# Splitting the k.k products from row 6 on into two f16 parts, in a fused feed-forward and delta-rule attention kernel

## What is computed

```
h = silu(tlin(x, w1)) * tlin(x, w2)            # 256 -> 1024
h = gelu(tlin(h, h1)); h = gelu(tlin(h, h2))   # 1024 -> 1024, weights -1, 0, 1, scaled by row
x = x + 0.5 * tlin(h, w3)                      # 1024 -> 256

k = k / max(norm(k), 1e-6)
for t in range(1024):                          # per batch and head, S is 16 x 16
    retrieval = S @ k[t]
    S = S + outer(beta[t] * (v[t] - retrieval), k[t])
    o[t] = S @ q[t]
x = x + o @ w_out + b_out
```

## Time and profile before

| what | us |
|---|---|
| median of three runs | 1911.45 (1910.48 to 1912.49) |
| the profiled execution | 1912.61 |
| its span, first to last instruction | 1910.6 |
| PE busy | 1789.6 |
| POOL busy | 1239.6 |
| DVE busy | 1167.3 |
| ACT busy | 1069.4 |
| granted TensorE clock, mean | 0.989 of full speed |

### The profile page before, as it was taken

One profiled execution on the slowest core, in us unless ns is written; L12 is line 12 of the kernel. 1 busy time (PEld: TensorE's weight loads), 2 busy tenths in 40 slices (PEclk: granted clock), 3 DMA queues, 4 the chain that ended last, 5 costly groups with the idle time before them and its releaser, 6 DMA issues.

```text
span 1910.6 us, 28212 instructions
## 1 busy us (share of the span) xinstructions
PE 1789.6 (94%) x9674; PEld 1064.2 (56%) x9674; DVE 1167.3 (61%) x2729; ACT 1069.4 (56%) x2049; POOL 1239.6 (65%) x1458
## 2 busy tenths in 40 slices
PE   5999989999999899998999989999799999998999
PEld 4865545555655455554655545455455555554577
DVE  5154666767766676665666656567667777776330
ACT  5656465465655664646556465554646556645455
POOL 6554584667584856748476594856758567658564
PEclk9999989999999999999999999999999999999999
DMA  7000000000000000000000000000000000000000
GB/s 292 23 1 1 1 1 1 1 1 2 0 2 1 23 1 23 1 1 1 1 23 0 1 1 1 23 1 1 1 1 1 1 1 12 1 12 1 1 12 12
DMA packets 5261, 23.06 MB, mean 12 GB/s; under 512 B 640, under 2 KB 1664, under 8 KB 3584
## 3 DMA queue, kind: packets, MB, share of 16 engines
q1 hardware_dynamic: 5120, 21.26, 3.0%
HBM read 17.06 MB, written 4.19 MB: 11 GB/s over the span
## 4 chain that ended last, share of the span: by engine, by line
PE 57%; POOL 23%; issue 8%; DVE 7%; ACT 4%; DMA 0%; POOLq 0%; ACTq 0%; SPq 0%; DVEq 0%
PE ffn_bank L1013 36%; POOL hid_lo L514 8%; POOL hid L523 6%; PE att_bank L1061 4%; PE att_bank L1051 4%; PE att_bank L1033 4%; POOL pairs L549 4%; POOL pairs_lo L557 3%; PE ffn_bank L996 2%; PE ln_bank L966 2%; PE state_bank L1069 2%; PE att_bank L1078 1%; ACT hid L642 1%; DVE qk_u L834 1%; DVE roots L772 1%
## 5 line engine op out<-in xcount | busy, mean ns | idle before, releaser
L1013 PE MATMUL ffn_bank<-hid_hi,w_sb 128*128 128x512 f16 (+1 forms) x2592 | 899.3, 358 | 27.9 <-ACT hid L629 17.7
L1013 PE MATMUL ffn_bank<-hid_lo,w_sb 128*128 128x512 f16 (+1 forms) x2592 | 898.6, 358 | 0.0
L514 POOL TENSOR_TENSOR hid_lo<-hid,hid_hi 128x512 f16<-128x512 f32 (+1 forms) x432 | 454.2, 1067 | 314.0 <-ACT hid_hi L613 313.8
L1013 PEld LDWEIGHTS ffn_bank<-hid_hi,w_sb 128*128 128x128 f16 x2592 | 263.3, 102 | 252.4 <-ACT hid L629 22.5
L549 POOL TENSOR_TENSOR pairs<-KQ 128x32 f32<-128x32 f32 (+15 forms) x496 | 327.2, 673 | 112.0 <-DVE KQ L797 72.9
L1013 PEld LDWEIGHTS ffn_bank<-hid_lo,w_sb 128*128 128x128 f16 x2592 | 255.3, 99 | 231.0 <-issue 30.6
L613 ACT CAST hid_hi<-hid 128x512 f16<-128x512 f32 (+1 forms) x432 | 231.7, 572 | 104.8 <-POOL hid L523 103.8
L642 ACT ACTIVATE hid<-ffn_bank,par_sb 128x512 f32<-128x512 f32 (+1 forms) x288 | 168.3, 635 | 148.4 <-PE ffn_bank L1013 147.5
L834 DVE TENSOR_TENSOR qk_u<-att_bank,U_sb 128x32 f32<-128x32 f32 (+15 forms) x256 | 111.3, 435 | 186.9 <-PE att_bank L1049 185.4
L996 PE MATMUL ffn_bank<-xn_hi,w_sb 128*128 128x512 f16 (+1 forms) x576 | 202.0, 360 | 16.3 <-ACT gate L624 8.9
L557 POOL TENSOR_TENSOR pairs_lo<-pairs,pairs_hi 128x32 f16<-128x32 f32 (+15 forms) x256 | 181.8, 714 | 36.7 <-ACT pairs_hi L690 36.6
(11 more groups left out here) (83 smaller groups left out, 2179.0 us busy)
## 6 DMA issues: line engine op xcount, KB each, us to landing
NK<-in_w SPq DMA_DIRECT2D x11, 1024.0 KB, 6.7
X<-in_x SPq DMA_DIRECT2D x7, 512.0 KB, 3.5
out<-X SPq DMA_DIRECT2D x7, 512.0 KB, 2.6
wqkvb_sb<-in_wqkvb SPq DMA_DIRECT2D x1, 1024.0 KB, 8.0
X<-in_x SPq DMA_DIRECT2D x2, 256.0 KB, 2.7
out<-X SPq DMA_DIRECT2D x2, 256.0 KB, 2.1
wout_sb<-in_wout SPq DMA_DIRECT2D x1, 256.0 KB, 8.9
par_sb<-in_par SPq DMA_DIRECT2D x1, 24.0 KB, 2.4
```

The lines of the kernel that those rows point to most:

```text
L514: pool.tensor_tensor(hid_lo[layer % 2][:, m, call.cols], hid[:, u % 3, call.cols], hid_hi[layer % 2][:, m, call.cols], ALU.subtract).then_ ...
L1013: mm = nc.tensor.matmul(ffn_ps(call, j), weight(name, kk, 2 * pair + i), v[:, kk, cols], start=kk == 0 and part == 0, stop=kk == KT_FF - 1 ...
```

## The change

Rows 6 to 15 of the k.k products go the way of the q.k products: they are made 9 ticks ahead instead of 4, cast by ACT, subtracted by POOL, and multiplied in two f16 matmuls by a new f16 matrix of minus ones. Rows 1 to 5 stay as they are. At one tick POOL now makes the pairs of split dots before those of unsplit ones. The buffers are the same.

```diff
+KK_SPLIT = 6
-SPLIT = {use: q for q, use in enumerate(u for u in DOTS if u[0] == "qk")}
+SPLIT = {use: q for q, use in enumerate(u for u in DOTS if u[0] == "qk" or u[2] >= KK_SPLIT)}
...
+        head_minus16 = sb("head_minus16", [P, P], F16)
...
-            pool.wait_ge(side_ready, 3)
+            pool.wait_ge(side_ready, 4)
...
-                for what, lead in PAIR_LEAD.items():
+                for whole, lead in ((False, PAIR_LEAD["qk"]), (True, PAIR_LEAD["kk"])):
                     for dot in dots_at(f, e + lead):
-                        if dot[0] == what:
+                        if (dot not in SPLIT) == whole:
                             make_pairs(dot)
...
+            nc.vector.tensor_scalar(head_minus16[:, :], head_ones[:, :], -1.0, None, ALU.mult).then_inc(side_ready, 1)
...
-                    i = SPLIT[dot]
-                    nc.tensor.matmul(ps[:, 0:n], head_ones16[:, :], pair(pairs_hi, i, dot), start=True, stop=False)
-                    nc.tensor.matmul(ps[:, 0:n], head_ones16[:, :], pair(pairs_lo, i, dot), start=False, stop=True).then_inc(att_filled, 1)
+                    i, ones = SPLIT[dot], head_ones16 if dot[0] == "qk" else head_minus16
+                    nc.tensor.matmul(ps[:, 0:n], ones[:, :], pair(pairs_hi, i, dot), start=True, stop=False)
+                    nc.tensor.matmul(ps[:, 0:n], ones[:, :], pair(pairs_lo, i, dot), start=False, stop=True).then_inc(att_filled, 1)
```

More of the change, by code:

```diff
@@ L724, in _ @@
             nc.vector.tensor_copy(head_ones16[:, :], head_ones[:, :]).then_inc(side_ready, 1)
+            nc.vector.tensor_scalar(head_minus16[:, :], head_ones[:, :], -1.0, None, ALU.mult).then_inc(side_ready, 1)
             dve.wait_ge(consts_ready, 2)
-            dve.wait_ge(side_ready, 3)
+            dve.wait_ge(side_ready, 4)
             nc.vector.memset(u_ps, 0.0).then_inc(u_zeroed, 1)
@@ L1108, in _ @@
             pe.wait_ge(masks_ready, 2)
-            pe.wait_ge(side_ready, 3)
+            pe.wait_ge(side_ready, 4)
             pe.wait_ge(u_zeroed, 1)
```

## The result

| | before | after |
|---|---|---|
| median of four runs, us | 1911.97 (1910.48 to 1913.47) | 1949.51 (1946.35 to 1949.60) |
| the profiled execution | 1912.61 | 1949.43 |
| its span | 1910.6 | 1947.7 |

The changed kernel takes 1.0192 times as long, interval 1.0175 to 1.0210. It is slower, as forecast, but the time lies above the range, 3.5 us over its upper end and 21.5 us over the value. A few executions of the study (one of e1, one of the kernel before) ran in a much slower state of the chip, at a lower granted clock; they are left out of all ratios and ranges.

A forecast was written before the change was run, and what follows sets the result against it. PE was taken as the bound on average, POOL in frames 3 and 13. To the profiled 1912.61 us the terms -0.7 + 0.2 + 2.6 - 0.4 + 1.5 + 12 add +15.2, giving 1928; range 1907 to 1946.

The forecast's parts named there:

- frame 6, from row 6 on: `xn_lo` stands in front of row 15's subtraction, so only row 15's own gain is left: -0.4 us.
- frame 4, from row 6 on: `xn_lo` stands in front of row 12's subtraction and delays PE, while rows 13 to 15 give 1.1: +1.5 us.
- frames 3 and 13: POOL is the bound there; the added subtractions delay PE's first q.k dot by some 6 us each, 12 us for both.
- PE's gain: Splitting k.k rows 6 to 15 saves PE 2.80 us per part, 44.8 us in 16 parts.
- What is added: Ten subtractions per part on POOL, 135 us in all, and ten casts on ACT, 75 us in all.
- Row 11 behind `xn_lo`: Row 11's subtraction follows `xn_lo` at tick 74; in frames 7 to 10 row 11 comes 1.55 us later than before.
- The step that failed: Rows 11 to 15 give PE 1.73 us per frame after row 11, if POOL keeps up.
- Three new waits of POOL on PE: Makes of rows 7, 8 and 9 wait for buffers of rows 3, 4 and 5; costed at nothing.
- The Trainium skill's rule: GpSimd and VectorE exclude each other during `xn` in 14 frames: 26 us in all, sum 1954; weighed at no cost.
- The much slower one: Rival: POOL and ACT hold PE in every part, 2 to 3 us more each, 1960 us; chance 0.14.
- delays are given back: No-change rival: delays in k.k rows only shorten later q.k waits in w1 and w2, 1913 to 1916; chance 0.12.
- The faster one: Rival: PE keeps its gain outside frames 3 and 13, 1885 us, or 1905 with half of it; chance 0.12.

The follow-up runs named there:

- e1: The changed kernel with `xn_lo` moved on POOL to tick 87, behind all k.k pairs, in twelve frames (not -1 and 4): 1922.01 us, ratio 1.0036.
- e3: The kernel before, nothing split, with the pairs of k.k row 11 made 3 ticks ahead instead of 4, behind `xn_lo`: 1942.69 us, ratio 1.0149.
- e2: The kernel before with `xn_lo` moved to tick 87 in the same frames as e1, nothing else: 1912.59 us, ratio 0.9990.
- e6: The changed kernel with the k.k products of frames 3 and 13 left unsplit: 1936.97 us, ratio 1.0124.
- e5: The changed kernel with ten unread f16 matmuls of 352 columns ahead of PE's wait for row 11 in twelve frames: 1946.64 us, ratio 1.0176.
- e9: The kernel before with the same ten filler matmuls as e5 in front of row 11 in the same twelve frames: 1923.45 us, ratio 1.0049.
- e4: The changed kernel with POOL's k.k subtractions cut to 32 columns, PE's work unchanged: 1918.38 us, ratio 1.0015.
- e8: The changed kernel with `xn_lo` late as in e1 and only frames 0, 1, 2, 6 to 10 and 14 split: 1903.65 us, ratio 0.9950.
- e10: e8 with casts and subtractions of the split k.k rows one tick earlier: 1902.22 us, ratio 0.9935 against the kernel before.

## Why the prediction failed, step by step

The distances between starts of PE's dots in the two timelines split the 37.1 us between them (each row is rounded by itself). "Twelve frames" are here those with `xn_lo` at tick 74: -1, 0, 1, 2, 5, 7 to 12 and 14.

| piece, us | predicted | measured |
|---|---|---|
| row 6 to row 11, twelve frames | +25.0 | +25.7 |
| row 11 to the first q.k dot, the same | -22.9 | -10.1 |
| frame 6, from row 6 on | -0.4 | -1.1 |
| frame 4, from row 6 on | +1.5 | +2.2 |
| frames 3 and 13 | +12 | +11.2 |
| rows 1 to 6, all frames | 0 | +6.6 |
| all between these stretches | 0 | +2.7 |
| sum | +15.2 | +37.1 |

(25.0 is 4 x 1.55, 3 x 1.80 and 5 x 2.67; -22.9 is 12 x -1.73 and the two waits of 1.05 for row 12.)

**PE's gain** was right: 44.8 predicted, 43.7 to 45.0 by the two ways of counting. The records of f32 k.k matmuls fell from 480 to 160:

```profile
L1054 PE MATMUL att_bank<-pairs,head_minus 128*128 128x32 f32 (+4 forms) x160 | 30.7, 275 | 0.7 <-POOL pairs L551 0.7
```

**What is added** was forecast a little too high: POOL +128 for 135, ACT +64 for 75. The widest subtraction took 1198 ns in the mean of both uses, where the earlier trace rows had 1292 for q.k alone:

```profile
L559 POOL TENSOR_TENSOR pairs_lo<-pairs,pairs_hi 128x192 f16<-128x192 f32 x32 | 17.6, 550 | 0.0
L559 POOL TENSOR_TENSOR pairs_lo<-pairs,pairs_hi 128x480 f16<-128x480 f32 x32 | 38.3, 1198 | 0.0
```

**Row 11 behind `xn_lo`** was right in place and size, with 25.7 us for 25.0 in twelve frames. e1 removes it in the eleven of them that it changes, e3 makes it without the split (24.3 us), and e2 bounds what moving `xn_lo` does otherwise at some 2 us.

**Frames 3 and 13** were right: 11.2 us in the timelines and 12.5 by e6, for 12. The distance from row 6 to row 15 grew from 20.4 us to 27.4 and 25.6 there, and was 25.1 in frames 7 to 10.

**The step that failed** is the sentence "Rows 11 to 15 (2080 columns) then give 1.73 us, if POOL keeps up; its list up to row 15 comes out within 0.3 us of PE's demand", carried from frame 7 to the eleven other frames. It held to 0.05 us in frames 7 to 10, each -1.78. The other eight gave -3.0 together instead of -16.0. e5 divides the 12.8 us that are missing in the twelve. With the filler, the same rows give -14.9 in twelve frames:

- 4.8 us go with the filler. 4.1 of them are in frames 0, 1 and 14, where PE waits 2.6 to 4.4 us for row 11 in after and works on at 1.2 GHz, and where e5 has no half clock. The prediction has no term for this, though the table of before lists the mean clock, 0.989. Frame -1 looks the same (-0.9), but there row 11 itself comes 1.2 us later in e5, so nothing is gained, and e9 shortens its tail as much (-1.1) without a half clock in it; this part is not shown to be the clock's.
- The other 8 us stay with the full clock. In frames -1, 5, 11 and 12 row 12 comes 3.1 to 4.1 us after row 11 in e5, against 2.0 in frames 7 to 10. POOL's timeline shows why: in these four two `hid_lo` stand between the two subtractions, and in the other eight they do not. e1 and e4 agree in part: with `xn_lo` gone (e1) PE still waits 2.40 and 3.81 us for row 12 in frames 5 and 12, though not in frame 11, and with short subtractions (e4) still 1.13 us in frame 5. No run moved the two `hid_lo` themselves, so this is read from the traces and not tested. That order could have been read before the result; I had read it in frame 7 only. These four give -1.1 us in e5 where 4 x -1.73 = -6.9 was predicted, so 5.8 of the 8; the rest is spread over frames 0, 1 and 2.

The ledger's 27.7 us for the clock are thus not its price. Part of what the clock takes, PE would have waited for POOL in any case: e5 took 19.5 us off the clock's row, and only some 3 us, no more than the noise, came off the time, with some 17 us of work added (as e9 shows), which was to cost nothing under its wait. The four executions of after say the same: at a mean clock of 0.975 and of 0.979, 8 us apart in the ledger, two of them took 1949.43 and 1949.60 us.

**Rows 1 to 6** were left out of the sum, since they are not split, and a second step failed here: "Three new waits of POOL on PE come too ... I cost them at nothing". POOL's waits for PE's matmuls before a make went from 39.1 us in 25 to 63.6 in 34. In frame 7 the one for row 7 was 1.87 us and did cost nothing. In frame 6 it does not. Between rows 5 and 6 PE takes a matmul of the layer norm (`ln_bank`) that waits for POOL's `roots`. Before, then after:

```profile
830.29 1.26 POOL L495 TENSOR_TENSOR roots<-X 128x512 f32<-128x512 f32 x1
831.61 1.13 PE L966 MATMUL ln_bank<-roots,average 128*128 128x512 f32 x2 [1.05 <-POOL roots L495]
```
```profile
851.67 0.67 POOL L551 TENSOR_TENSOR pairs<-KQ 128x256 f32<-128x256 f32 x1 [0.96 <-PE att_bank L1054]
855.02 1.27 POOL L497 TENSOR_TENSOR roots<-X 128x512 f32<-128x512 f32 x1
856.35 2.05 PE L969 MATMUL ln_bank<-roots,average 128*128 128x512 f32 x2 [1.96 <-POOL roots L497]
```

In front of `roots` now stand the makes of two more rows, POOL's wait of 0.96 us for PE to let go of a buffer, and a subtraction. PE waits 1.96 us instead of 1.05, and 3.4 us at half clock come with it, which the doubled duration shows (2.05 for 1.13). The piece grew by 2.6 us; in e5, with the same wait and no half clock, by 0.9. In frame 4 PE's wait for the same step rose from 2.36 to 2.83 us, since one more make stands in front of it, and 6.8 us at half clock come with it instead of 3.4; the piece grew by 1.8. These two frames make 4.4 of the 6.6 us. Of the rest some may be no effect of the split: in e2 and e3, where nothing is split, rows 1 to 6 took 1.5 us more as well, 1.2 of it in frame -1. The 2.7 us between the stretches were not taken apart.

**The Trainium skill's rule** on GpSimd and VectorE (SBUF — State Buffer, "SBUF: two separate sides") was weighed at no cost. The subtraction of row 10 (width 320), begun at 984.39 beside VectorE's `xn` of 983.66 to 985.51, took 1.77 us in frame 7, where this width took 0.79 in the mean before:

```profile
984.39 1.77 POOL L559 TENSOR_TENSOR pairs_lo<-pairs,pairs_hi 128x320 f16<-128x320 f32 x1
```

PE waited 0.9 us for it in frames 7 to 10. In after that cost nothing, as row 11 set the time behind it. In e1 and e8 it is what is left: these frames gain 1.8 us where the split is worth 2.8. By the rule as the prediction priced it, 26 us would have come on top; the traces show about 1 us in such a frame, and that hidden behind row 11 in after.

**The rivals.** The much slower one (POOL and ACT hold PE in every part, 1960) described part of what happened in eight frames, where PE waits for row 12 as well or goes on at half clock; in frames 7 to 10 it waits for rows 10 and 11 alone. That delays are given back in later waits did not come: the pieces between the stretches grew by 2.7 us. The faster one's upper value, 1905, is reached only by e8 and e10, which split nine parts and move `xn_lo`.

## What to carry to other kernels

When work moves from a full engine to one that works through a list in order, go through that list frame by frame, past the first late item to the second and third; one frame that fits says nothing of those whose list has another order. Go through it ahead of the changed rows too, since work moved forward delays what stands behind it there. A wait of the matrix engine in the middle of a busy stream can cost more than its length, because the clock may fall with it (1.70 us more in frame 1 of e3 than in frame 2); so keep the ledger of work, idle time and clock, and test its rows by an experiment, since they replace one another. And a change that is a loss as a whole may be a gain where the receiving engine has room: nine of sixteen parts, with `xn_lo` moved, give 0.5 to 0.65% (e8, e10).

## What was not expected of the hardware

The granted clock fell to 1.2 GHz behind single waits in the middle of a stream that was else full. Half-clock stretches within the span were 41.0 us in nine places before, 95.6 in 21 after, 58.7 in 13 with the filler. Behind the waits of 1.4 to 1.6 us in frames 7 to 10 it never fell, in after as in e3; with those of 2.7 to 4.0 us in frames 11, 12 and 14 of e3 it did, in the last two before the wait was over. The length of the wait does not decide it: of 3.13 and 3.14 us in frames 1 and 2 of e3 only the first was followed by a fall, and in after one of 2.58 us (frame 0) was, and those of 2.61 and 2.62 us (frames 5 and 2) were not. What does decide it is not settled by these runs.

The Trainium skill (TensorE: Matmul & The Clock Gate, "HAM oscillation — how this bites in real kernels") counts half of the time at the lower clock as lost and shows it for a kernel that stalls on DMA between short bursts. The trace agrees on the half: in frame 11 of after matmuls of 512 columns stand 0.43 us apart at the lower clock and 0.22 at the full one. Here the same happens behind one wait for another engine, amid thousands of matmuls, and e5 shows that such a loss may cost nothing where another engine sets the pace.
